# A recurrent second layer on one core: nine of ten GpSimd sums per round moved to VectorE

## The chip, the cores and the metric

The kernel runs on one core of a Trainium2 chip, in float32 throughout. The metric is the device time of one execution in microseconds (us). The core's engines are TensorE (PE in the profile), VectorE (DVE), ScalarE (ACT), GpSimd (POOL) and SyncE (SP), which issues most of the DMAs. Each engine runs its own list of instructions in order; between engines only semaphores order the work.

## What is computed

The reference has two layers, over a batch of 8 sequences of 256 tokens and 512 channels. The first is a transformer block (self attention, cross attention, feed-forward). The change doesn't touch it. The second is a recurrent block with a time mix and a channel mix. Cut to what matters:

```
xa  = layernorm(x)                        # xaT: channels on partitions
sx  = previous token of xa - xa
xxx = tanh((xa + sx * maa_x) @ maa_w1) @ maa_w2      # five mixes
x_f = xa + sx * (maa_stack_f + xxx_f)     # f = k, w, v, r, g
w = exp(-exp(..)); r, k, v = x_r @ Wr.T, x_k @ Wk.T, x_v @ Wv.T; g = silu(x_g @ Wg.T)
for each token: out = r . (u * k v + S);  S = k v + w * S
og = group_norm(out);  x1 = x + (og * g) @ Wo.T
xc = layernorm(x1);  sx2 = previous token of xc - xc
out = x1 + sigmoid((xc + sx2 * maa_r) @ Wfr.T) * (square(relu((xc + sx2 * maa_k) @ Wfk.T)) @ Wfv.T)
```

## The kernel before

The second layer (`recurrent_block`) is a pipeline over batches with five stages, "lfasd": `l` is the layer norm ahead of the first layer's feed-forward, `f` that feed-forward (64 matmuls of 256 columns and 32 of 512 per batch), `a` the time mix up to r, k, v, w and g, `s` the scan with the group norm and the output product, `d` the channel mix. `pipeline` (L1476) calls each engine's `body` once per round. In round i the stages work on batches i, i-1, i-2, i-3 and i-4, so that rounds 2 and 3 lack the late stages, rounds 4 to 7 have all five, round 8 lacks `l`, round 9 also lacks `f`, and rounds 10 and 11 are the end. In the trace round 2 begins at about 850 us, round 3 at 970, round 4 at 1113, and rounds 4 to 8 take some 141 us each, to 1819.

The order of work in a round is written out by hand, separately for each engine. A tensor of one batch lies as 128 partitions x 4 x 256, so that one sum over it is one instruction of 128x1024 elements.

**GpSimd** (L1706 to L1755) makes ten such sums per round, each behind a wait on another engine's semaphore: `xf = x2 + b2` (L1731); `sx` from `xaT` (L1736); the five mix sums `mixed += xaT` (`add_xa`, L1714), the first four in a loop; `o += bv`, the scan's output plus the bonus of the same token (L1744); then the fifth mix sum; `o *= sq`, the group norm's rstd (L1750); and `sx2` from `xcT` (L1753). Where stage `f` is absent (round 9), VectorE makes the fifth mix sum (L2354) and `o *= sq` (L2373) itself; in round 10 also `sx2` (L2285).

**VectorE** (L2110 to L2409) runs the scan in eight steps of a batch, `step(s, 0)` to `step(s, 7)` (L2124): a product (L2133) of 128x2048, two scans (L2144) of 128x1028 and a product (L2151) of 128x2048. Steps 0 to 2 of a batch come at the end of one round, steps 3 to 7 in the next. Between the steps stand the small operations: `shift` (L2154) makes `sx * (stack + xxx)` into `mixed`, from PSUM; L2313 makes the input of the first mix product from `sx`; L2357 is k * r for the bonus; L2364 the gate; L2368 the bonus times v; L2379 the gated output; `take_ff2` (L2240) adds a feed-forward product from PSUM into `xf` and so frees one of two banks; `mix_channel` (L2271) uses `sx2`.

**TensorE** (L1957) runs through the products of all stages in one list. In the tail of a round it makes the feed-forward product L1795, then the product `dev` of `o` (L1847, waits on `o_made`, L2065), the first half of the gate product (L1828, waits on the fifth mix sum, L2053), the product `var` (L1847), the second half of the gate, the bonus in two halves (L1847, L2078; the second half needs the bank that VectorE's first L2364 frees), a feed-forward product (L1805), the sums of a scan step (`add_rows`, L1897) and the output product. The k product waits on mix sum 1 (L2008), the v product on mix sum 3 (L2034).

**ScalarE** squares the deviations, makes rstd (L2644, L2647), the gate's tanh (L2527), then waits for `o*sq` (L2651) and scales it (L2653). SyncE reads `o` back from memory (L1653) once the scan's rows are stored, loads the scan's rows `ks`, `ws`, `rs`, `vs` and the weights, which are streamed anew in each round.

Of the kernel before, what the change touches and what calls it, by code (L numbers as in the profile page):

```python
# [6 lines left out]
ALU = mybir.AluOpType  # L7
# [1202 lines left out]
def recurrent_block(nc, sems, T, keep, x2_dram, x3_dram, out_dram, early_ring_in, early_x3_out):  # L1210


    with ExitStack() as ctx:
# [493 lines left out]
        def _(pool):  # L1707
# [3 lines left out]
            def add_xa(a, f):  # L1711
                pool.wait_ge(*emptied(a, f"mix{f}", 1))
                alone(pool)
                nc.gpsimd.tensor_tensor(mixed[:, f % 2, :, :], mixed[:, f % 2, :, :], xaT[:, :, 1:SEQ + 1], ALU.add)\  # L1714
                    .then_inc(mix_made.sem, 1)

            def body(t):
# [15 lines left out]
                if a is not None:  # L1733
                    pool.wait_ge(*emptied(a, "xaT", 1))
                    alone(pool)
                    nc.gpsimd.tensor_tensor(sx[:, :, :], xaT[:, :, 0:SEQ], xaT[:, :, 1:SEQ + 1], ALU.subtract)\  # L1736
                        .then_inc(sx_made.sem, 1)
                    for f_ in range(4):
                        add_xa(a, f_)
                if s is not None and f is not None:  # L1740
                    for tally in (bv_in, o_in):
                        pool.wait_ge(tally.sem, tally.at(s, 1))
                        alone(pool)
                    nc.gpsimd.tensor_tensor(o[:, :, :], o[:, :, :], bv[:, :, :], ALU.add).then_inc(o_made.sem, 1)  # L1744
                if a is not None and f is not None:
                    add_xa(a, 4)
                if s is not None and f is not None:
                    pool.wait_ge(rstd_made.sem, rstd_made.at(s, 1))
                    alone(pool)
                    nc.gpsimd.tensor_tensor(o[:, :, :], o[:, :, :], sq[:, :, :], ALU.mult).then_inc(y_made.sem, 1)  # L1750
                    pool.wait_ge(*emptied(s, "xcT", 1))
                    alone(pool)
                    nc.gpsimd.tensor_tensor(sx2[:, :, :], xcT[:, :, 0:SEQ], xcT[:, :, 1:SEQ + 1], ALU.subtract)\  # L1753
                        .then_inc(sx2_made.sem, 1)
# [356 lines left out]
        def _(dve):  # L2111
# [158 lines left out]

            def mix_channel(s):  # L2271
# [22 lines left out]
            def body(t):  # L2294
# [28 lines left out]
                if a is not None:  # L2323
                    shift_pair(a, (0, 1), 1)
                if d is not None and d != LAST:
                    add_channel(d)
# [406 lines left out]
```

## Time and profile before

| | |
|---|---|
| median of 3 runs | 2054.96 us (2052.15 to 2056.28) |
| the profiled execution | 2053.13 us, its span 2051.4 us |
| PE busy | 1899.5 us (93%) |
| DVE busy | 1445.3 us (70%) |
| ACT busy | 870.5 us (42%) |
| POOL busy | 486.0 us (24%) |
| POOL in the second layer: L1714 | 39 instructions, 114.2 us |
| L1731, L1736, L1744, L1750, L1753 | 7, 8, 6, 6, 6 instructions |

How to read it: busy time is the sum over the instructions of an engine, and a share of the span is an average over two layers with different limits. The median of all runs lies 1.8 us above the profiled execution. In a row of a timeline or a group, L1714 is a line of the kernel, `b_mixed<-b_mixed,b_xaT` the tensor written and those read, `128x1024` partitions by elements, and "[3.95 <-POOL b_mixed L1714]" the idle time ahead of the instruction and what ended it. Records of neighbouring instructions can overlap by some 0.1 us. "issue" is waiting for nothing that the profile shows. A row of the windows gives: stretch, its length, then busy us and (x instructions) of PE, PEld (weight loads), DVE, ACT and POOL, the granted TensorE clock as a share of full speed, the DMA share and GB/s.

### The profile page before, as it was taken

The numbers are of one execution on the slowest core, as the hardware profiler recorded it, in microseconds if no ns is written. First come the engines' busy times: TensorE is split into PE (matmuls) and PEld (weight loads), VectorE is DVE, ScalarE is ACT, GpSimd is POOL, SyncE is SP. The second block draws the span as 40 slices with busy tenths as digits, with TensorE's granted clock in tenths as the row PEclk, the third lists the DMA queues.
The fourth block names the chain that finished last, engine by engine and source line by source line (L and its number), as shares of the span: only waits on it lengthen the run. The fifth ranks groups of instructions, "written<-read, shape, count | busy, mean of one in ns | idle before, by whom it ended". The sixth has DMA issues, their size and how long they took to land.

```text
span 2051.4 us, 29340 instructions
## 1 busy us (share of the span) xinstructions
PE 1899.5 (93%) x11284; PEld 1293.4 (63%) x11284; DVE 1445.3 (70%) x2472; ACT 870.5 (42%) x2068; POOL 486.0 (24%) x234
## 2 busy tenths in 40 slices
PE   6789999999999999989799999999999999997577
PEld 4566666667666666566576666766767766766343
DVE  3366666767666635236968978888889889789972
ACT  2466666666666656221243243242332431321222
POOL 2233333343433322120221211212202202112000
PEclk9799999999999999999899999999999999999788
DMA  7000000101001021643554464563644644625330
GB/s 216 19 9 27 11 27 12 32 7 36 27 11 47 32 88 42 209 168 113 180 189 157 154 203 141 187 204 126 209 169 162 213 160 138 205 101 166 113 103 31
DMA packets 152788, 227.80 MB, mean 111 GB/s; under 512 B 24185, under 2 KB 72057, under 8 KB 152649
## 3 DMA queue, kind: packets, MB, share of 16 engines
q1 hardware_dynamic: 127272, 205.07, 30.4%
q10 hardware_dynamic: 25376, 20.86, 3.2%
q8 instruction: 90, 1.47, 0.3%
q14 instruction: 50, 0.40, 0.1%
HBM read 183.94 MB, written 41.96 MB: 110 GB/s over the span
## 4 chain that ended last, share of the span: by engine, by line
PE 44%; DVE 6%; DMA 3%; issue 2%; ACT 2%; POOL 1%; ACTq 1%; DVEq 0%; SPq 0%; POOLq 0%
PE b_f_bank L1805 9%; PE b_f_bank L1795 9%; PE b_a_bank L1828 7%; PE b_c_bank L1838 7%; PE b_c_bank L1828 3%; DVE b_ring L2144 2%; PE b_y_bank L1897 2%; PE b_a_bank L1861 2%; DMA b_o<-b_o_all 1%; POOL b_mixed L1714 1%; DVE b_ring L2133 1%; DMA b_o_all<-b_osum 1%; PE b_f_bank L1925 1%; ACTq L2466 1%; PE b_a_bank L1882 1%
## 5 line engine op out<-in xcount | busy, mean ns | idle before, releaser
L406 POOL TENSOR_TENSOR a_prob<-a_prob,a_rowinv 128x1024 f32<-128x1024 f32 x128 | 242.2, 1893 | 504.7 <-DVE a_rowinv L861 504.6
L1093 ACT ACTIVATE a_prob<-a_score,a_low 128x256 f32<-128x256 f32 x512 | 253.6, 497 | 228.1 <-DVE a_low L853 228.1
L2144 DVE TENSOR_TENSOR_SCAN b_ring<-b_ws,b_ring 128x1028 f32<-128x1028 f32 x128 | 312.4, 2482 | 3.6 <-ACT b_ring L2449 0.7
L1795 PE MATMUL b_f_bank<-k_hT_early,k_w_early 128*128 128x256 f32 x896 | 208.9, 388 | 3.9 <-DVE k_enc_early L2248 2.5
L1805 PE MATMUL b_f_bank<-k_w_early 128*128 128x512 f32 x448 | 204.3, 607 | 0.0
L853 DVE CUSTOM_DVE_ANT_0 a_score<-a_score,a_fill 128x256 f32<-128x256 f32 x512 | 196.6, 446 | 4.8 <-DVE a_score L840 0.2
L1795 PEld LDWEIGHTS b_f_bank<-k_hT_early,k_w_early 128*128 128x128 f32 x896 | 169.4, 192 | 40.7 <-issue 18.3
L840 DVE SCALAR_TENSOR_TENSOR a_score<-a_S,a_mask 128x1024 f32<-128x1024 f32 x128 | 150.7, 1219 | 49.5 <-PE a_S L600 49.5
L1714 POOL TENSOR_TENSOR b_mixed<-b_mixed,b_xaT 128x1024 f32<-128x1024 f32 x39 | 114.2, 2945 | 299.9 <-DVE b_mixed L2170 279.6
L2133 DVE TENSOR_TENSOR b_ring<-b_ks,b_vs 128x2048 f32<-128x2048 f32 x64 | 180.4, 2820 | 3.2 <-issue 3.2
L833 DVE TENSOR_SCALAR a_ctxT<-a_O,a_vec 128x256 f32<-128x256 f32 x64 | 31.0, 484 | 207.6 <-PE a_O L630 207.6
L2151 DVE TENSOR_TENSOR b_ring<-b_ring,b_rs 128x2048 f32<-128x2048 f32 x64 | 153.8, 2403 | 2.2
L1805 PEld LDWEIGHTS b_f_bank<-k_w_early 128*128 128x128 f32 x448 | 84.8, 193 | 102.1 <-issue 101.7
L614 PEld LDWEIGHTS a_S<-k_ident,a_prob 128*128 128x128 f32 x1024 | 120.6, 145 | 30.9 <-issue 15.3
L614 PE MATMUL a_S<-k_ident,a_prob 128*128 128x128 f32 x1024 | 127.9, 280 | 9.9 <-DVE a_score L840 9.9
L1105 ACT ACTIVATE a_probT<-a_S 128x1024 f32<-128x1024 f32 x128 | 128.5, 1007 | 7.8 <-PE a_S L614 7.8
L1828 PE MATMUL b_a_bank<-b_mixed,b_shared 128*128 128x256 f32 x512 | 117.5, 389 | 7.9 <-DMA b_shared<-in_Wk_dram 3.5
L501 PE MATMUL a_G<-k_hT_early,k_w_early 128*128 128x256 f32 x512 | 118.7, 386 | 4.9 <-ACT k_hT_early L1047 3.7
L1828 PEld LDWEIGHTS b_a_bank<-b_mixed,b_shared 128*128 128x128 f32 x512 | 99.8, 196 | 23.1 <-issue 7.7
L2508 ACT ACTIVATE k_w_early<-b_f_bank,k_b_col 128x256 f32<-128x256 f32 x112 | 46.9, 470 | 156.5 <-PE b_f_bank L1795 156.4
L501 PEld LDWEIGHTS a_G<-k_hT_early,k_w_early 128*128 128x128 f32 x512 | 96.5, 193 | 21.4 <-issue 8.8
L1093 ACT ACTIVATION_READ_ACCUMULATOR a_prob<-a_score,a_low 128x1 f32 x512 | 96.8, 189 | 0.0
(201 smaller groups left out, 3004.0 us busy)
## 6 DMA issues: line engine op xcount, KB each, us to landing
k_w_early<-in_w_dram SPq DMA_DIRECT2D x64, 1024.0 KB, 5.5
b_vs<-b_v_all SPq DMA_DIRECT2D x32, 512.0 KB, 5.0
b_shared<-in_Wv_dram SPq DMA_DIRECT2D x8, 1024.0 KB, 6.1
b_shared<-in_Wk_dram SPq DMA_DIRECT2D x8, 1024.0 KB, 5.3
b_shared<-in_Wo_dram SPq DMA_DIRECT2D x8, 1024.0 KB, 6.1
b_shared<-in_Wfk_dram SPq DMA_DIRECT2D x8, 1024.0 KB, 7.9
b_shared<-in_Wfv_dram SPq DMA_DIRECT2D x8, 1024.0 KB, 5.3
b_w_all<-b_wT ACTq DMA_DIRECT2D x8, 514.0 KB, 4.4
```

The source lines that it names most:

```text
L406: nc.gpsimd.tensor_tensor(two, two, inv.to_broadcast([P, 2 * TT, SEQ]), ALU.mult)\
L501: last = nc.tensor.matmul(bank[:, m * SEQ:(m + 1) * SEQ], w[:, c, col + m * P:col + (m + 1) * P], actT[:, c, :], start=(c == 0), stop=(c = ...
L614: last = nc.tensor.transpose(S[:, j, k * SEQ + a * P:k * SEQ + (a + 1) * P], prob[:, HPG * (g % 2) + j, a * SEQ + k * P:a * SEQ + (k + 1) ...
L840: last = nc.vector.scalar_tensor_tensor(out=score[:, 2 * pair:2 * pair + 2, :], in0=S[:, 2 * pair:2 * pair + 2, :], scalar=-SCORE_SCALE, i ...
L853: last = nc.vector.tensor_tensor_reduce(sc, sc, fill[:, at, a * SEQ:(a + 1) * SEQ], 1.0, 3.0e38, ALU.add, ALU.min, low[:, HPG * g + j, a:a ...
L1093: last = nc.scalar.activation(prob[:, slot, a * SEQ:(a + 1) * SEQ], score[:, j, a * SEQ:(a + 1) * SEQ], ACT.Exp, bias=low[:, head, a:a + 1 ...
L1795: last = nc.tensor.matmul(bank[:, m * SEQ:(m + 1) * SEQ], w1[:, cg, col_:col_ + P], hTf[:, cg, :], start=(cg == 0), stop=(cg == CG - 1))
L1805: last = nc.tensor.matmul(bank[:, :], f1T(quarter, cg)[:, at * P:(at + 1) * P], w2[:, cg, :], start=(cg == 0), stop=(cg == CG - 1))
L1828: last = nc.tensor.matmul(tile(name, k)[:, m * SEQ:(m + 1) * SEQ], w[:, c, (2 * k + m) * P:(2 * k + m + 1) * P], act[:, c, :], start=(c == ...
L2133: nc.vector.tensor_tensor(slot[:, :, :, 1:SEQ + 1], ks[:, :, :].unsqueeze(1).to_broadcast([P, JCOLS, IROWS, SEQ]), vs[:, u // 2 % 2, u % 2 ...
L2144: last = nc.vector.tensor_tensor_scan(x_, flat(ws[:, :, :]), x_, 0.0, ALU.mult, ALU.add)
L2151: nc.vector.tensor_tensor(x_, x_, rs[:, :, :].unsqueeze(1).to_broadcast([P, JCOLS, IROWS, SEQ]), ALU.mult).then_inc(weighed.sem, 1)
```

## The change

VectorE makes nine of the ten sums, each directly behind the operation whose result it needs: `sx` after step 3, mix sums 1 and 2 after the second pair of shifts of mixes 0 and 1, mix sums 3 and 4 after those of mixes 2 and 3 (ahead of step 7), the fifth mix sum after its shift, `o += bv` after L2357 and ahead of step 0, `o *= sq` after step 0 and ahead of the gate, `sx2` ahead of `mix_channel`. GpSimd keeps `xf = x2 + b2` (L1731). The semaphores stay the same ones; the waits that stood in GpSimd's queue stand in VectorE's. No other engine's list changes.

```diff
--- before.py
+++ after.py
@@ -1708,12 +1708,6 @@
             nc.gpsimd.memset(wT[:, :, 0:1], 0.0)
             xf_made.done(pool, 1)
 
-            def add_xa(a, f):
-                pool.wait_ge(*emptied(a, f"mix{f}", 1))
-                alone(pool)
-                nc.gpsimd.tensor_tensor(mixed[:, f % 2, :, :], mixed[:, f % 2, :, :], xaT[:, :, 1:SEQ + 1], ALU.add)\
-                    .then_inc(mix_made.sem, 1)
-
             def body(t):
                 l, f, a, s, d = t.stages()
 
@@ -1730,28 +1724,6 @@
                         alone(pool)
                     nc.gpsimd.tensor_tensor(xf[:, :, :], x2[:, :, :], b2_all[:, :, :].to_broadcast([P, TT, DM]), ALU.add)\
                         .then_inc(xf_made.sem, 1)
-                if a is not None:
-                    pool.wait_ge(*emptied(a, "xaT", 1))
-                    alone(pool)
-                    nc.gpsimd.tensor_tensor(sx[:, :, :], xaT[:, :, 0:SEQ], xaT[:, :, 1:SEQ + 1], ALU.subtract)\
-                        .then_inc(sx_made.sem, 1)
-                    for f_ in range(4):
-                        add_xa(a, f_)
-                if s is not None and f is not None:
-                    for tally in (bv_in, o_in):
-                        pool.wait_ge(tally.sem, tally.at(s, 1))
-                        alone(pool)
-                    nc.gpsimd.tensor_tensor(o[:, :, :], o[:, :, :], bv[:, :, :], ALU.add).then_inc(o_made.sem, 1)
-                if a is not None and f is not None:
-                    add_xa(a, 4)
-                if s is not None and f is not None:
-                    pool.wait_ge(rstd_made.sem, rstd_made.at(s, 1))
-                    alone(pool)
-                    nc.gpsimd.tensor_tensor(o[:, :, :], o[:, :, :], sq[:, :, :], ALU.mult).then_inc(y_made.sem, 1)
-                    pool.wait_ge(*emptied(s, "xcT", 1))
-                    alone(pool)
-                    nc.gpsimd.tensor_tensor(sx2[:, :, :], xcT[:, :, 0:SEQ], xcT[:, :, 1:SEQ + 1], ALU.subtract)\
-                        .then_inc(sx2_made.sem, 1)
             pipeline(pool, body)
 
         @block.tensor
@@ -2268,6 +2240,11 @@
                 nc.vector.scalar_tensor_tensor(out=x_, in0=flat(o[:, :, :]), scalar=0.5, in1=x_, op0=ALU.mult,
                                                op1=ALU.add).then_inc(out_made.sem, 1)
 
+            def add_xa(a, f):
+                dve.wait_ge(*emptied(a, f"mix{f}", 1))
+                nc.vector.tensor_tensor(mixed[:, f % 2, :, :], mixed[:, f % 2, :, :], xaT[:, :, 1:SEQ + 1], ALU.add)\
+                    .then_inc(mix_made.sem, 1)
+
             def mix_channel(s):
 
                 dve.wait_ge(sx2_made.sem, sx2_made.at(s, 1))
@@ -2307,6 +2284,9 @@
                 if s is not None:
                     step(s, 3)
                 if a is not None:
+                    dve.wait_ge(*emptied(a, "xaT", 1))
+                    nc.vector.tensor_tensor(sx[:, :, :], xaT[:, :, 0:SEQ], xaT[:, :, 1:SEQ + 1], ALU.subtract)\
+                        .then_inc(sx_made.sem, 1)
                     dve.wait_ge(sx_made.sem, sx_made.at(a, 1))
                     dve.wait_ge(g_out.sem, g_out.at(a, 0))
                     for cg in range(CG):
@@ -2322,6 +2302,8 @@
                     gate_channel(d)
                 if a is not None:
                     shift_pair(a, (0, 1), 1)
+                    add_xa(a, 0)
+                    add_xa(a, 1)
                 if d is not None and d != LAST:
                     add_channel(d)
                 if s is not None:
@@ -2334,6 +2316,8 @@
                     take_ff2(f, 0)
                 if a is not None:
                     shift_pair(a, (2, 3), 1)
+                    add_xa(a, 2)
+                    add_xa(a, 3)
                 if s is not None:
                     if f is None and a is not None:
                         step(s, 6)
@@ -2349,13 +2333,17 @@
                 if a is not None:
                     for k in range(2):
                         shift(a, 4, k)
-                    if f is None:
-                        dve.wait_ge(*emptied(a, "mix4", 1))
-                        nc.vector.tensor_tensor(mixed[:, 0, :, :], mixed[:, 0, :, :], xaT[:, :, 1:SEQ + 1], ALU.add)\
-                            .then_inc(mix_made.sem, 1)
+                    add_xa(a, 4)
                     dve.wait_ge(*emptied(a, "r", 1))
                     nc.vector.tensor_tensor(mixed[:, 1, :, :], kT[:, :, :], rT[:, :, :], ALU.mult).then_inc(rk_made.sem, 1)
+                    if s is not None and f is not None:
+                        for tally in (bv_in, o_in):
+                            dve.wait_ge(tally.sem, tally.at(s, 1))
+                        nc.vector.tensor_tensor(o[:, :, :], o[:, :, :], bv[:, :, :], ALU.add).then_inc(o_made.sem, 1)
                     step(a, 0)
+                    if s is not None and f is not None:
+                        dve.wait_ge(rstd_made.sem, rstd_made.at(s, 1))
+                        nc.vector.tensor_tensor(o[:, :, :], o[:, :, :], sq[:, :, :], ALU.mult).then_inc(y_made.sem, 1)
                     if f is None:
                         step(a, 1)
                     for k in range(2):
@@ -2399,6 +2387,9 @@
                 if f is not None:
                     take_ff2(f, 4)
                 if s is not None and f is not None:
+                    dve.wait_ge(*emptied(s, "xcT", 1))
+                    nc.vector.tensor_tensor(sx2[:, :, :], xcT[:, :, 0:SEQ], xcT[:, :, 1:SEQ + 1], ALU.subtract)\
+                        .then_inc(sx2_made.sem, 1)
                     mix_channel(s)
                 if f is not None:
                     for i in range(5, 8):
```

## Rows read from the trace of the kernel before

**Rows 1.** Windows, rounds 4 to 8 (columns as in the section on time)

```profile
1113.00:1254.30 141.30, 139.41 (x809) 96.23 (x808) 119.46 (x108) 47.10 (x89) 27.44 (x10) 1.00 0.54 175
...
sum 706.30, PE 696.85 PEld 480.92 DVE 593.81 ACT 230.82 POOL 140.32; mean PE 139.37 PEld 96.18 DVE 118.76 ACT 46.16 POOL 28.06
```

**Rows 2.** PE's waits in rounds 4 to 8: us in total, times, longest

```profile
PE b_a_bank L1828 <- POOL b_mixed L1714: 5.6, 5, 1.1
PE b_a_bank L1847 <- DVE b_z_gT L2364: 3.1, 5, 0.6
```

**Rows 3.** Chain in round 4, from 1196 to 1222: start us, us, what

```profile
1200.91 3.16 POOL b_mixed L1714
...
1204.12 3.72 PE b_a_bank L1828 x16
...
1213.75 0.70 DVE b_z_gT L2364
...
1214.50 1.13 PE b_a_bank L1847 x4
```

**Rows 4.** POOL timeline, round 4: start, us, instruction, [idle <-releaser]

```profile
1198.61 2.35 POOL L1744 TENSOR_TENSOR b_o<-b_o,b_bv 128x1024 f32<-128x1024 f32 x1 [19.44 <-DMA b_o<-b_o_all]
...
1213.38 2.35 POOL L1750 TENSOR_TENSOR b_o<-b_o,b_sq 128x1024 f32<-128x1024 f32 x1 [9.31 <-ACT b_sq L2647]
```

**Rows 5.** DVE's timeline in round 4

```profile
1194.17 0.17 DVE L2191 RECIPROCAL b_rstd<-b_std 128x2 f32<-128x2 f32 x1 [6.19 <-ACT b_std L2420]
...
1197.30 2.16 DVE L2162 SCALAR_TENSOR_TENSOR b_mixed<-b_a_bank,k_vec_b,b_sx 128x128 f32<-128x128 f32 x8 [1.92 <-PE b_a_bank L1873]
1199.37 2.67 DVE L2357 TENSOR_TENSOR b_mixed<-b_kT,b_rT 128x1024 f32<-128x1024 f32 x1
1201.96 4.25 DVE L2133 TENSOR_TENSOR b_ring<-b_ks,b_vs 128x2048 f32<-128x2048 f32 x1
```

**Rows 6.** DVE timeline, round 9, where it makes such a sum already

```profile
1893.77 1.22 DVE L2354 TENSOR_TENSOR b_mixed<-b_mixed,b_xaT 128x1024 f32<-128x1024 f32 x1
1894.91 1.22 DVE L2357 TENSOR_TENSOR b_mixed<-b_kT,b_rT 128x1024 f32<-128x1024 f32 x1
```

**Rows 7.** DVE L2133 over the whole run: ns min/median/max

```profile
L2133 DVE TENSOR_TENSOR b_ring<-b_ks,b_vs x64: 2274/2284/4254, 919.7 to 1980.2; 128x2048 f32<-128x2048 f32 x64
```

**Rows 8.** PE's timeline in round 2: waits, and what ran after them

```profile
924.03 9.81 PE L1828 MATMUL b_a_bank<-b_mixed,b_Wg 128*128 128x256 f32 x32 [3.95 <-POOL b_mixed L1714]
...
935.40 3.60 PE L1805 MATMUL b_f_bank<-k_w_early 128*128 128x512 f32 x8
...
949.60 5.38 PE L1795 MATMUL b_f_bank<-k_hT_early,k_w_early 128*128 128x256 f32 x16 [2.50 <-DVE k_enc_early L2248]
```

**Rows 9.** DVE's timeline in rounds 2 and 3

```profile
928.36 2.29 DVE L2151 TENSOR_TENSOR b_ring<-b_ring,b_rs 128x2048 f32<-128x2048 f32 x1
...
984.48 3.80 DVE L2151 TENSOR_TENSOR b_ring<-b_ring,b_rs 128x2048 f32<-128x2048 f32 x1
```

**Rows 10.** PE's timeline in round 3

```profile
1025.01 2.07 PE L1861 MATMUL b_a_bank<-b_t,b_maa_w 32*128 32x256 f32 x8 [7.48 <-DVE b_mixed L2170]
...
1060.52 1.99 PE L1847 MATMUL b_c_bank<-b_o,k_dev_head 128*128 128x256 f32 x8 [1.93 <-POOL b_o L1744]
```

**Rows 11.** DVE's timeline in round 9, steps 6 and 7

```profile
1868.06 3.75 DVE L2133 TENSOR_TENSOR b_ring<-b_ks,b_vs 128x2048 f32<-128x2048 f32 x1
1871.85 6.35 DVE L2144 TENSOR_TENSOR_SCAN b_ring<-b_ws,b_ring 128x1028 f32<-128x1028 f32 x2
...
1882.76 4.49 DVE L2144 TENSOR_TENSOR_SCAN b_ring<-b_ws,b_ring 128x1028 f32<-128x1028 f32 x2
```

**Rows 12.** PE's timeline in round 9, wait for step 6

```profile
1880.58 1.08 PE L1897 MATMUL b_y_bank<-b_ring,k_same_quad 128*32 128x128 f32 x32 [3.69 <-DVE b_ring L2151]
```

**Rows 13.** PE's timeline in round 9, third idle time

```profile
1914.98 1.27 PE L1847 MATMUL b_a_bank<-b_mixed,k_u_head 128*128 128x256 f32 x4 [1.94 <-DVE b_z_gT L2364]
1916.19 1.93 PE L1897 MATMUL b_y_bank<-b_ring,k_same_quad 128*32 128x128 f32 x32
```

## The prediction

> **What bounds the kernel now.** I cut the second layer into rounds with the windows first. Rounds 4 to 8 are alike: 706.3 us in all, TensorE busy for 696.9 of it at full granted clock, VectorE for 593.8 [rows 1]. TensorE is the bound there, VectorE has 141.3 - 119.5 = 21.8 us idle per round. Whatever VectorE gains in these rounds is therefore worth nothing by itself; only what TensorE waits for counts. Its list of waits for the same stretch is short [rows 2]: 1.1 us per round for GpSimd's fifth mix sum (L1714), 0.6 us per round for VectorE's gate (L2364), and one of 0.2 us. All five waits on L1714 are this one, so mix sums 1 to 4, `sx`, `sx2` and `o*sq` are waited for by nobody on TensorE. The chain of waits shows where the two sit: the tail of the round, between the fifth mix sum and the bonus product [rows 3]. Rounds 2, 3 and 9 are different: there VectorE's scan steps are waited for, for 7.48 us in round 3 and 3.69 us in round 9 [rows 10, 12], and GpSimd's fifth sum alone for 3.95 us in round 2 [rows 8].
>
> **The price of one sum.** GpSimd takes 2.35 us where nothing is in its way [rows 4]. VectorE makes the same shape in 1.22 us, and the next starts 1.14 us after it [rows 6]. Nine of these put 9 x 1.14 = 10.3 us per round on VectorE.
>
> **What VectorE gets back.** Its product L2133 takes 2.28 us, but 4.25 us when a GpSimd sum is under way [rows 5, 7]; a pair of scans takes 4.49 us, but 6.35 us beside two sums [rows 11]; L2357 takes 2.67 us instead of 1.22 [rows 5, 6]. One engine waits for the other's instruction to end. The Trainium skill says the same of the shared port ("SBUF — State Buffer", Who interferes with whom). In a round like 4, three L2133, one scan pair, L2357 and one more operation of its shape meet the nine sums: I estimate 2.0 + 1.5 + 2.0 + 1.9 + 1.4 + 1.4 = 10.2 us. So VectorE's load stays nearly as it is and fits in its time; even if nothing came back, 10.3 us would fit in 21.8. The tenth sum stays on GpSimd and still holds VectorE up once a round.
>
> A rule speaks against the change: the Trainium skill ("Perfetto Trace Analysis", Optimizing Scalar/DVE Operations) has saturated VectorE hand work over to other engines. VectorE idles for 21.8 us a round here, so the rule does not bite; were VectorE the bound and nothing given back, five rounds would grow by 5 x 10.3 = 52 us, against the 7.5 of the sum below.
>
> **The tail of rounds 4 to 8, on round 4's times.**
> - Before: TensorE starts the deviation product at about 1201.0, when GpSimd's `o+bv` (1198.61 + 2.35) is done, which is also when it is free; GpSimd then makes the fifth mix sum until 1204.07, and the gate product starts at 1204.12 [rows 3, 4].
> - After: VectorE's L2162 ends at 1199.46; then the fifth mix sum (1199.5), L2357 (1200.6) and only then `o+bv` (1201.8 to 1203.0) [rows 5, 6]. The deviation product starts at 1203.05, 2.05 us later: a new wait. It takes 1.8 us, so the gate product, whose input is long ready, starts at 1204.9: 0.8 us later than before.
> - ScalarE's variance and rstd follow TensorE and come 0.8 us later too. GpSimd started `o*sq` at 1213.38 [rows 4], so VectorE starts it at 1214.1 and ends at 1215.3. Step 0 isn't late: it starts at 1202.9 without the 1.97 us of holding and ends at 1212.1. `y` is ready at 1215.3 against 1215.7 before, so ScalarE isn't late.
> - But `o*sq` now stands ahead of the gate L2364, which started at 1213.75 and now starts at 1215.2. The second bonus product waits for it: 1214.50 becomes 1215.95. So the delay is 1.45 us, and it stays to the end of the round, because TensorE never catches up. VectorE does not carry its own delay over: it waits for ScalarE for 6.19 us before the next tail [rows 5].
>
> Five rounds by 1.5 us: **+7.5 us**.
>
> **Other placements.** `sx` (L1736) runs after step 3 for 1.14 us on VectorE instead of overlapping it; step 3's L2151 was held for 1.5 us in return (3.80 against 2.29) [rows 9]. Mix sums 1 to 4 follow their shifts, ahead of steps 5 and 7: +2.3 us for each pair, against the holding of 1.5 + 1.9 that went. `sx2` puts 1.14 us ahead of two second-layer sums that free PSUM banks; TensorE has about 1 us in hand there, so I cost it at zero, and at most 0.2 us per round if that cover is gone. VectorE's own waits now stand in its queue: the one on the load of `o` is met at 1198.6 in round 4, 3 us before it is asked for [rows 4]. No DMA is added or moved; queues of SP and POOL lose nothing but the nine sums.
>
> **Round 2** loses the 3.95 us wait, and the half-clock stretch after it. But the scan step that follows (L2151 ends at 930.65) then decides the gate and the second bonus product [rows 9]: VectorE's L2364 ends near 930.7, TensorE's second-layer product of 935.40 starts near 931.9 [rows 8]. That is 3.5 us earlier, or 1.8 if the clock falls in the new 2.9 us wait: after a wait of 2.50 us sixteen matmuls took 5.38 us [rows 8] against 3.7 at full clock. With 0.4 us at the first mix sum I take **-3.0 us** (bounds -2.2 and -4.0).
>
> **Round 3**: VectorE sets the pace until the 7.48 us wait [rows 10]. `sx` and step 3 give -0.4, the first pair of mix sums 2.3 - 3.4 = -1.1: -1.4 in all. The tail costs less than later (the input `o` came late, TensorE waited 1.93 us already [rows 10]): +0.6. Sum **-0.8 us**.
>
> **Round 9**: the same two terms, -0.4 and 2.3 - 1.5 - 1.9 = -1.1, ahead of a chain of steps that VectorE carries to the end [rows 11, 12]: **-1.6 us**. Rounds 10 and 11 have no such sums.
>
> **The clock.** The trace shows no cost of the new 2.05 us wait, so it is bounded. Nothing: after 1.93 us the matmuls ran at full clock [rows 10]. Up to 1.7 us each: after 2.50 us they ran at half clock (1.2 instead of 2.4 GHz) [rows 8]. Between them, after 1.94 us, the y products took 1.93 us instead of 1.1 [rows 13], about 1.0 us in all. I take one loss of 1.0 us in five rounds, since 1.93 and 1.94 are the nearest rows and differ; range 0 to 8.5.
>
> **Sum:** 7.5 - 3.0 - 0.8 - 1.6 + 1.0 = +3.1 us. It is made against the profiled execution (2053.1 us, span 2051.4); the median of three runs is 2055.0, so I forecast 2058.
>
> **Rivals.**
> - *Clock lost in most tails* (slower). The place is the deviation product's wait; the price 1.0 to 1.7 us each, decided once the wait is over about 2 us. Four or five losses give 7.5 - 5.4 + 4 to 8.5 = +6 to +11, 2061 to 2066. For it: rows 8 and 13; against: rows 10. Chance 0.24.
> - *The holding was the true price* (faster). If round 2 gives its full 4.0 with the clock kept and more, round 3 and 9 give the 3.4 us of each pair in full, and the tail costs 0.7 us per round because the gate isn't pushed back: 3.5 - 4 - 2.5 - 2.5 = -5.5, 2049.5. Against it: L2364 stands behind `o*sq` in VectorE's queue, whatever happens before. Chance 0.10.
> - *VectorE becomes the bound* or the load of `o` comes later than 1201.8: its queue, step 0 behind it, would stop. +5 us or more, 2060 to 2065. Against it: 21.8 us idle, 3 us in hand. Chance 0.09.
> - *Nothing moves* (the two sides cancel, GpSimd's waits were the whole cost): within 2 us of 2055. Chance 0.12.
> - The forecast: 0.45.
>
> A measurement of this kernel can tell about 0.2% (4.1 us) from no change. My forecast is inside it, with its upper third outside, so it gives 0.15 to slower; with the rivals: faster 0.12, same 0.46, slower 0.42. The range leaves out the far ends: 2050 to 2066.
>
> **What would show it.** In rounds 4 to 8, TensorE's waits: about 2.0 us at L1847 for `o+bv` and 1.3 us for L2364, none for a mix sum; round length 143.0. L2133 at 2.28 us at all but one place, no scan pair at 6.35 us except beside the tenth sum. GpSimd has seven sums left. PEclk in rounds 4 to 8 near 1.0; a tenth below 1.0 there is the first rival. Round 2 shorter by 3 us. I am wrong if TensorE's new waits sum to under 2.5 us per round, or if VectorE is never idle in one.

## The result, and the profile after

| | before | after |
|---|---|---|
| median of 19 runs each | 2053.71 us (2052.02 to 2058.07) | 2058.93 us (2055.31 to 2066.32) |
| the profiled execution | 2053.13 us | 2064.26 us, its span 2062.5 us |

The ratio is 1.0027, 95% interval 1.0018 to 1.0037: slower by 5 us. That is little, but the interval leaves out 1. The profiled execution lies 5.3 us above its own kernel's median, and after's runs spread over 11 us where before's spread over 6. So a term read in this one profile has to be held against the other runs before it is believed.

The page of after, busy time by engine:

```profile
## 1 busy us (share of the span) xinstructions
PE 1903.0 (92%) x11284; PEld 1298.6 (63%) x11284; DVE 1450.2 (70%) x2537; ACT 870.7 (42%) x2068; POOL 307.7 (15%) x169
```

GpSimd lost 65 instructions and 178 us. VectorE gained 65 instructions and 4.9 us. That is all its load grew. In lines of after, L2245 is a mix sum, L2342 `o+bv`, L2346 `o*sq`, L2338 the old L2357, L2352 the gate (old L2364), L2105 the old L2133, L2123 the old L2151, L1819 the deviation and bonus products (old L1847), L1800 the old L1828, L1877 the old L1905.

Windows of after on rounds 4 to 8, the same columns as [rows 1]:

```profile
1096.70:1239.50 142.80, 139.34 (x813) 96.50 (x809) 119.60 (x118) 47.14 (x91) 3.15 (x1) 1.00 0.55 174
...
1382.20:1526.70 144.50, 141.04 (x814) 97.62 (x809) 119.62 (x118) 47.15 (x90) 3.33 (x1) 0.99 0.52 172
...
1669.50:1813.00 143.50, 140.04 (x804) 96.76 (x801) 116.06 (x111) 43.92 (x88) 3.44 (x1) 0.99 0.51 168
sum 716.30, PE 699.00 PEld 483.83 DVE 594.28 ACT 232.38 POOL 17.57; mean PE 139.80 PEld 96.77 DVE 118.86 ACT 46.48 POOL 3.51
```

Five rounds take 716.3 us instead of 706.3. VectorE is busy for 594.28 us of them against 593.81 [rows 1]: nine more sums a round, and no more load. TensorE's busy time grew only in the two rounds with a granted clock of 0.99.

What TensorE waits for in rounds 4 to 8 of after, in the form of [rows 2]:

```profile
PE b_c_bank L1819 <- DVE b_o L2342: 10.6, 5, 2.1
PE b_a_bank L1819 <- DVE b_z_gT L2352: 6.3, 5, 1.3
```

No mix sum is waited for any more. `o+bv` is, for 2.1 us in every round, and the wait for the gate doubled from 0.62 to 1.27 us. VectorE's timeline of round 4 shows why:

```profile
1195.00 2.16 DVE L2134 SCALAR_TENSOR_TENSOR b_mixed<-b_a_bank,k_vec_b,b_sx 128x128 f32<-128x128 f32 x8 [1.93 <-PE b_a_bank L1845]
1197.19 1.23 DVE L2245 TENSOR_TENSOR b_mixed<-b_mixed,b_xaT 128x1024 f32<-128x1024 f32 x1
1198.34 1.22 DVE L2338 TENSOR_TENSOR b_mixed<-b_kT,b_rT 128x1024 f32<-128x1024 f32 x1
1199.47 1.22 DVE L2342 TENSOR_TENSOR b_o<-b_o,b_bv 128x1024 f32<-128x1024 f32 x1
1200.61 2.29 DVE L2105 TENSOR_TENSOR b_ring<-b_ks,b_vs 128x2048 f32<-128x2048 f32 x1
...
1211.62 1.23 DVE L2346 TENSOR_TENSOR b_o<-b_o,b_sq 128x1024 f32<-128x1024 f32 x1 [1.62 <-ACT b_sq L2638]
1212.76 1.28 DVE L2352 SCALAR_TENSOR_TENSOR b_z_gT<-b_z_gT,b_a_bank 128x512 f32<-128x512 f32 x2
```

`o+bv` stands third behind the shifts, and the gate stands behind `o*sq`, which waits for ScalarE. Nothing is held: the fifth sum, L2338 and `o+bv` take 1.22 us each, where L2357 took 2.67 beside GpSimd [rows 5]. TensorE, rounds 4, 6 and 8, at the deviation product:

```profile
1200.74 1.99 PE L1819 MATMUL b_c_bank<-b_o,k_dev_head 128*128 128x256 f32 x8 [2.13 <-DVE b_o L2342]
...
1486.28 3.38 PE L1819 MATMUL b_c_bank<-b_o,k_dev_head 128*128 128x256 f32 x8 [2.12 <-DVE b_o L2342]
...
1773.51 3.63 PE L1819 MATMUL b_c_bank<-b_o,k_dev_head 128*128 128x256 f32 x8 [2.13 <-DVE b_o L2342]
```

The same wait, three times. After it the eight matmuls take 1.99 us, or 3.4 to 3.6 us at a lower clock: in rounds 6 and 8 full clock was lost. The window on the slow matmuls of round 6 has the granted clock, 0.50 of full speed:

```profile
1486.70:1490.10 3.40, 3.40 (x10) 2.66 (x9) 3.27 (x2) 1.00 (x2) 0.00 (x0) 0.50 0.42 154
```

**Where the 11.1 us of span went.** I cut both traces at the first matmul of the longest run (x32) of the feed-forward product L1805 (L1777 in after) in each round, so that round 4 goes from 1099.0 to 1240.5 before. The first layer and its end gave +1.3, round 2 -4.0, round 3 +0.4, rounds 4 to 8 +9.8, and rounds 9 to 11 +3.6 us. A clean round took 142.77 us against 141.49, which is 5 x 1.28 = 6.4; the two rounds without full clock took 1.7 more each, 3.4 together. The medians differ by 5.2 us only: 11.1 less the 3.6 of the last rounds (which other profiles of the same list do not show, see below) and the 1.3 of a layer that the change does not touch would be 6.2.

### The profile page after: what moved, and what is told of

It reads as the page before. It is cut to its first block, busy times and chain, and to the rows that moved or that the text cites. A ratio compares the mean times of both kernels' runs of the same rounds, so it can differ in the third digit from the quotient of the medians.

```text
span 2062.5 us, 29275 instructions
## 1 busy us (share of the span) xinstructions
PE 1903.0 (92%) x11284; PEld 1298.6 (63%) x11284; DVE 1450.2 (70%) x2537; ACT 870.7 (42%) x2068; POOL 307.7 (15%) x169
## 4 chain that ended last, share of the span: by engine, by line
PE 44%; DVE 7%; DMA 3%; issue 2%; ACT 2%; ACTq 1%; SPq 0%; DVEq 0%
PE b_f_bank L1777 9%; PE b_f_bank L1767 8%; PE b_c_bank L1810 8%; PE b_a_bank L1800 7%; PE b_c_bank L1800 3%; DVE b_ring L2116 2%; PE b_y_bank L1869 2%; DMA b_vs<-b_v_all 2%; PE b_a_bank L1833 2%; PE b_c_bank L1819 1%; DVE b_ring L2105 1%; DMA b_o_all<-b_osum 1%; PE b_f_bank L1897 1%; ACTq L2457 1%; PE b_a_bank L1854 1%
## 5 line engine op out<-in xcount | busy, mean ns | idle before, releaser
L2116 DVE TENSOR_TENSOR_SCAN b_ring<-b_ws,b_ring 128x1028 f32<-128x1028 f32 x128 | 298.0, 2370 | 3.6 <-ACT b_ring L2440 0.7
L1777 PE MATMUL b_f_bank<-k_w_early 128*128 128x512 f32 x448 | 204.4, 607 | 0.0
L2123 DVE TENSOR_TENSOR b_ring<-b_ring,b_rs 128x2048 f32<-128x2048 f32 x64 | 148.7, 2323 | 2.6 <-DMA b_rs<-b_r_all 0.5
L1777 PEld LDWEIGHTS b_f_bank<-k_w_early 128*128 128x128 f32 x448 | 84.9, 194 | 102.4 <-issue 102.0
L2105 DVE TENSOR_TENSOR b_ring<-b_ks,b_vs 128x2048 f32<-128x2048 f32 x64 | 146.3, 2286 | 0.4 <-issue 0.4
L1725 POOL TENSOR_TENSOR k_enc_early<-k_x_early,k_b_all 128x1024 f32<-128x1024 f32 x7 | 22.9, 3271 | 821.8 <-DMA x_all<-k_enc_early 821.8
L1800 PE MATMUL b_a_bank<-b_mixed,b_shared 128*128 128x256 f32 x512 | 118.3, 391 | 7.1 <-DMA b_shared<-in_Wk_dram 3.4
L1800 PEld LDWEIGHTS b_a_bank<-b_mixed,b_shared 128*128 128x128 f32 x512 | 100.4, 197 | 22.5 <-issue 7.2
```

Of the source, the lines that this page charges most:

```text
L1777: last = nc.tensor.matmul(bank[:, :], f1T(quarter, cg)[:, at * P:(at + 1) * P], w2[:, cg, :], start=(cg == 0), stop=(cg == CG - 1))
L1800: last = nc.tensor.matmul(tile(name, k)[:, m * SEQ:(m + 1) * SEQ], w[:, c, (2 * k + m) * P:(2 * k + m + 1) * P], act[:, c, :], start=(c == ...
L2105: nc.vector.tensor_tensor(slot[:, :, :, 1:SEQ + 1], ks[:, :, :].unsqueeze(1).to_broadcast([P, JCOLS, IROWS, SEQ]), vs[:, u // 2 % 2, u % 2 ...
L2116: last = nc.vector.tensor_tensor_scan(x_, flat(ws[:, :, :]), x_, 0.0, ALU.mult, ALU.add)
```

## The experiments

All edits are to the changed kernel. Ratios are against the kernel before, run beside each on the same chip. "Round" is a round of rounds 4 to 8, cut as above. "OBV" stands for the wait on `bv` and `o` with `o += bv`, "OSQ" for the wait on rstd with `o *= sq`.

**1. `o+bv` first (e1_o_first).**

```diff
                     for k in range(2):
                         shift(a, 4, k)
+                    OBV
                     add_xa(a, 4)
                     ...
-                    OBV
                     step(a, 0)
```

> The change with one line moved: VectorE makes o += bv ahead of the fifth mix sum instead of behind that sum and L2357. Theory (order in the tail): o is loaded before the shift of the fifth mix ends, so the sum is done when TensorE is free and its wait of 2.1 us at the deviation product goes; the wait for the gate stays near 1.3 us. Rounds 4 to 8: 142.8 - 1.9 = about 140.9 us each and full clock there; time 2047 to 2051, ratio to the kernel before 0.997 to 0.999. Rival (load): VectorE has too much to do, the place of one sum changes nothing but moves the wait to the gate product; rounds stay at 142.8, ratio 1.002 to 1.003.

Measured: 2048.54 us, ratio 0.9971 (0.9954 to 0.9989). The wait at the deviation product is gone in all rounds, and rounds take 140.3 to 141.2 us but for one of 142.88. The other wait grew:

```profile
PE b_a_bank L1819 <- DVE b_z_gT L2352: 9.6, 5, 2.1
```

TensorE arrives earlier, and the gate still stands behind `o*sq`, so this wait, expected to stay near 1.3 us, grew by 0.4 to 0.8 us. Full clock, expected throughout, was lost after it twice: in round 3 (a wait of 2.26 us) and in round 5 (2.09 us, the round of 142.88), but not after the 2.10 and 2.08 us of rounds 4 and 8. Moving one operation by two places in one queue is worth 0.6% (1.0027 to 0.9971).

**2. `o+bv` and `o*sq` back to GpSimd (e4_two_back).** The two blocks go back into GpSimd's list, in their old order; the other seven sums stay on VectorE.

> The change with o += bv and o *= sq given back to GpSimd; the other seven sums stay on VectorE. Theory (order in the tail): both new waits go, and the old wait of 1.1 us for the fifth mix sum stays away, since GpSimd no longer makes it: rounds 4 to 8 at 140.2 to 140.5 us each, waits of TensorE there 0.6 us for the gate alone; ratio 0.994 to 0.997 (2041 to 2048 us). Rival (load): seven more sums on VectorE still cost something in each round, and GpSimd's sums hold VectorE up again: rounds at 141.5 or more, ratio 1.000 to 1.002.

Measured: 2040.30 us, ratio 0.9935 (0.9922 to 0.9948), rounds of 139.2 to 140.6. Its waits in rounds 4 to 8 (L1828 is its L1819, L2354 its gate):

```profile
PE b_a_bank L1828 <- DVE b_z_gT L2354: 3.1, 5, 0.6
PE b_c_bank L1828 <- POOL b_o L1731: 0.6, 1, 0.6
```

Without the mix sums in front of it GpSimd has `o+bv` ready nearly in time, and the wait for the gate is the 0.6 of before. The ratio is a little better than expected (0.994 to 0.997). A clean round, 140.03 us, is still 0.3 us longer than the best version's below: the deviation product takes 1.99 us there as after a wait, not the 1.89 us of a product that follows without a break.

**3. The tail alone (e5_tail_only).** Only the fifth mix sum, `o+bv` and `o*sq` on VectorE; the other six go back to GpSimd.

> Only the tail's three sums move to VectorE (fifth mix sum, o += bv, o *= sq); sx, mix sums 1 to 4 and sx2 stay on GpSimd. Theory (order in the tail): rounds 4 to 8 as slow as with the whole change, +1.3 us each and some with a clock loss of 1.7 us on top; round 2 still 3.6 us shorter; ratio 1.002 to 1.004. Rival (load): most of the loss comes from the six other sums; rounds near 141.5, ratio below 1.000.

Measured: 2061.68 us, ratio 1.0034 (1.0021 to 1.0047): as slow as the whole change. Rounds of 142.77 us (141.90 in round 8), waits of 2.13 and 1.26 us, and one round of 144.46 in which full clock was lost. Round 2 was 5.6 us shorter than before, not the 3.6 expected; 1.7 of it is the clock in its first product, which ran in 7.14 us instead of before's 8.83.

**4. The head alone (e6_head_only).** The reverse: `sx`, mix sums 1 to 4 and `sx2` on VectorE, the tail's three on GpSimd.

> Only sx, mix sums 1 to 4 and sx2 move to VectorE; the tail's three stay on GpSimd. Theory (order in the tail): rounds 4 to 8 unchanged at 141.5 us with the old waits of 1.1 and 0.6 us, round 2 shorter by 0.4 us only; ratio 0.999 to 1.001. Rival (load): these six sums carry most of the loss, rounds at 142 or more; ratio 1.002 or more.

Measured: 2053.71 us, ratio 0.9993 (0.9984 to 1.0001): no change beyond its interval. Rounds of 140.5 to 141.9 us but for one of 146.06, with the waits of before:

```profile
PE b_a_bank L1814 <- POOL b_mixed L1735: 6.6, 5, 2.2
PE b_a_bank L1833 <- DVE b_z_gT L2360: 3.1, 5, 0.6
PE b_c_bank L1833 <- POOL b_o L1731: 2.4, 2, 1.9
```

Four of the five waits for the fifth sum (its L1735) are the 1.1 us of [rows 2]. In the long round TensorE waited 1.9 us for GpSimd's `o+bv` and then 2.2 us for the fifth sum behind it; after the first wait the matmuls kept full clock (1.99 us), after the second they ran at half clock (5.41 us for sixteen, against 3.72). Round 2 was 2.2 us shorter, of which 1.7 is again the clock in its first product. Experiments 3 and 4 together put the whole price on the tail, and there on order, since the tail's work is the same in 3 and in the best version below.

**5. All nine on VectorE, in a better order (e3_both).** `o+bv` ahead of the fifth sum, and `o*sq` between the two halves of the gate.

```diff
                     step(a, 0)
-                    OSQ
                     ...
                     for k in range(2):
                         ...
                         nc.vector.scalar_tensor_tensor(out=x_, in0=x_, scalar=1.0, in1=tile("g", k)[:, :],
                                                        op0=ALU.add, op1=ALU.mult).then_inc(empty_sem("g"), 1)
+                        if k == 0:
+                            OSQ
```

> All nine sums on VectorE as in the change, but two of them placed otherwise: o += bv ahead of the fifth mix sum, o *= sq behind the first of the two gates L2364. Theory (order in the tail): VectorE's speed at these sums was never the trouble, so with nine sums on VectorE the rounds 4 to 8 fall to 139.8 to 140.3 us, as with the two sums given back to GpSimd; TensorE waits 0.6 us for the gate only; ratio 0.993 to 0.996 (2040 to 2046 us). Rival: the two sums belong on GpSimd, VectorE can't hold both without one of them being late; rounds at 140.8 or more and ratio 0.997 or more.

Measured: 2038.99 us (2038.63 to 2043.58), ratio 0.9924 (0.991 to 0.9937), a little better than expected (0.993 to 0.996) and the fastest version, with e12; e4's interval overlaps theirs. A clean round takes 139.73 us. VectorE's timeline of its round 4 (L2339 is `o+bv`, L2349 the gate, L2353 `o*sq`):

```profile
1193.89 1.22 DVE L2339 TENSOR_TENSOR b_o<-b_o,b_bv 128x1024 f32<-128x1024 f32 x1
1195.02 1.22 DVE L2245 TENSOR_TENSOR b_mixed<-b_mixed,b_xaT 128x1024 f32<-128x1024 f32 x1
1196.16 1.22 DVE L2342 TENSOR_TENSOR b_mixed<-b_kT,b_rT 128x1024 f32<-128x1024 f32 x1
...
1206.54 0.69 DVE L2349 SCALAR_TENSOR_TENSOR b_z_gT<-b_z_gT,b_a_bank 128x512 f32<-128x512 f32 x1
1207.14 1.22 DVE L2353 TENSOR_TENSOR b_o<-b_o,b_sq 128x1024 f32<-128x1024 f32 x1
1208.28 0.68 DVE L2349 SCALAR_TENSOR_TENSOR b_z_gT<-b_z_gT,b_a_bank 128x512 f32<-128x512 f32 x1
```

TensorE, same stretch, and the sum of the windows on its five rounds:

```profile
1195.27 1.89 PE L1819 MATMUL b_c_bank<-b_o,k_dev_head 128*128 128x256 f32 x8
...
1207.28 1.13 PE L1819 MATMUL b_a_bank<-b_mixed,k_u_head 128*128 128x256 f32 x4 [0.62 <-DVE b_z_gT L2349]
```

```profile
sum 698.30, PE 694.32 PEld 481.51 DVE 593.67 ACT 232.54 POOL 15.78; mean PE 138.86 PEld 96.30 DVE 118.73 ACT 46.51 POOL 3.16
```

VectorE's busy time is that of before and of after to within 0.1%, in five rounds that are 8 us shorter than before and 18 shorter than after. Its load decided nothing; the place of two operations did. TensorE idles for 4.0 us in five rounds instead of the 9.5 of before; the gate is waited for, 0.6 us in three rounds and 0.94 and 0.84 in two.

**6 and 7. One of the two alone on GpSimd (e9_sq_back, e10_obv_back).** OSQ, or OBV, moved to GpSimd's list, all else as after.

> The change with o *= sq alone given back to GpSimd. It separates the two new waits. Theory: the wait of 2.1 us at the deviation product stays, the wait for the gate goes back from 1.3 to 0.6 us; rounds 4 to 8 at 142.1 us where the clock holds, and the clock is still lost in some; ratio 1.000 to 1.003. Rival (the second wait follows from the first): the gate wait stays near 1.3 us and the rounds at 142.8.

> The change with o += bv alone given back to GpSimd. Theory: the wait at the deviation product goes; the wait for the gate grows to about 1.7 us, because o *= sq still stands ahead of it; rounds 4 to 8 at 140.8 us; ratio 0.996 to 0.999. Rival: the deviation product still waits, since GpSimd's sum and VectorE's hold each other up; rounds at 142 or more.

Measured: with OSQ back 2057.41 us, 1.0009 (1.0 to 1.0018); clean rounds 142.12, that is 0.65 less than after, and waits of 2.13 and 0.62 us. Three rounds lost full clock (143.8 us). With OBV back 2047.93 us, 0.9968 (0.9956 to 0.998); rounds of 140.5 to 141.4, the gate is waited for, 1.6 to 1.9 us, and in one round GpSimd's `o+bv`, 0.36 us. No round lost full clock. So `o*sq` ahead of the gate costs 0.65 us a round, or 1.0 to 1.5 where TensorE comes early (e10, e1).

**8. The same change with the wait shorter or longer (e13, e11, e14).** e13 puts `o+bv` between the fifth sum and L2338, a place earlier than after. e11 puts one dummy product ahead of it, which writes `sx2` (free there), e14 two:

```diff
+                        for dummy in (sx, sx2):
+                            nc.vector.tensor_tensor(dummy[:, :, :], kT[:, :, :], rT[:, :, :], ALU.mult)
                         OBV
```

> The change with o += bv between the fifth mix sum and L2357, so that the deviation product's wait is about 1.0 us instead of 2.1. Theory (the clock is lost the more often the longer the wait): no loss in rounds 3 to 8; these rounds take 141.6 us all alike; ratio 0.997 to 1.000. Rival (the losses don't depend on this wait): one to three rounds of the profile with the deviation product at 2.7 to 3.8 us instead of 2.0.

> The change with one more product of 128x1024 on VectorE ahead of o += bv (it writes sx2, which is made anew before it is read; nothing else changes). The wait at the deviation product becomes 2.1 + 1.15 = 3.3 us in rounds 3 to 8. Theory of the clock (a wait of 2.1 us loses it in some rounds, one of 2.5 us or more always does): every one of these rounds runs its next matmuls at half clock, so rounds 4 to 8 take 142.8 + 1.15 + 1.7 = 145.6 us, all alike; ratio 1.008 to 1.011. Rival (the losses in two rounds of the profile have another cause, as the weights or the DMAs of those rounds): most rounds take 143.9, a few 145.7; ratio 1.004 to 1.007.

> The change with two more products of 128x1024 on VectorE ahead of o += bv (they write sx and sx2, which are made anew before they are read). The deviation product's wait becomes 4.4 us. Theory: with a wait this long the clock is lost in all six rounds; rounds 4 to 8 take 142.8 + 2.3 + 1.7 to 1.9 = about 147 us; ratio 1.012 to 1.016. Rival: as with 3.3 us, two rounds or more of six keep the full clock, at 145 us.

Each of these has six such waits, rounds 3 to 8. "Lost" counts those after which the eight matmuls took 2.7 us or more instead of 1.99. The medians are of 10, 19, 4 and 2 runs, the rest is from one profile per kernel:

| kernel | wait, us | lost | round, clean / lost | median us | ratio |
|---|---|---|---|---|---|
| e13 | 0.99 | 0 of 6 | 141.64 / none | 2050.27 | 0.9979 (0.9969 to 0.9988) |
| after, e5, e9 | 2.13 | 2, 1 and 3 of 6 | 142.77 / 144.46 (after) | 2058.93 (after) | 1.0027 (1.0018 to 1.0037) |
| e11 | 3.26 | 4 of 6 | 143.91 / 145.6 to 146.6 | 2074.85 | 1.0092 (1.0075 to 1.0108) |
| e14 | 4.40 | 6 of 6 | none / 146.73 | 2085.15 | 1.0145 (1.0121 to 1.0169) |

TensorE in round 4 of e14:

```profile
1208.73 3.66 PE L1819 MATMUL b_c_bank<-b_o,k_dev_head 128*128 128x256 f32 x8 [4.40 <-DVE b_o L2345]
1212.22 3.62 PE L1800 MATMUL b_a_bank<-b_mixed,b_Wg 128*128 128x256 f32 x16
```

The first dummy adds its own 1.14 us to a clean round. A loss adds 1.7 us, and in rounds 7 and 8 of e11 2.7 to 2.8 us: in round 7 the eight matmuls took 3.78 us and the gate product's sixteen behind them 4.62 instead of 3.62. My expectation for e11 that a wait longer than about 2.5 us always loses the clock fell, though its ratio lay in the range: at 3.26 us two of six kept full clock. At 2.13 us 6 of 18 lost it. e5 and e9 are other kernels with the same wait, and one profile of each is few; the order of the four lines is what is shown, not the odds themselves, and what decides between two equal waits stays open.

**9. The second broadcast load of round 9 later (e12_second_part_later).** In the profile of after, two transfers of round 9 took longer from issue to landing than before:

```profile
b_r_all<-b_rT ACTq DMA_DIRECT2D x1, 512.0 KB, 7.8
b_o_all<-b_osum ACTq DMA_DIRECT2D x4, 128.0 KB, 4.9
```

Before, the same rows of the DMA issues:

```profile
b_r_all<-b_rT ACTq DMA_DIRECT2D x1, 512.0 KB, 5.3
b_o_all<-b_osum ACTq DMA_DIRECT2D x4, 128.0 KB, 2.9
```

The load of `o` can only start behind these stores. In after the store of `r` was issued 1.2 us behind the two loads of `vs`, before 2.9 us behind them, so that more of it ran beside them. So e12 takes e3 and moves the second of them behind the load of `o`:

```diff
-                def load_begin():
+                def load_begin(parts=(0, 1)):
                 ...
-                    load_part(a, 0)
-                    load_part(a, 1)
+                    for part in parts:
+                        load_part(a, part)
                 ...
                 if a is not None and f is None:
-                    load_begin()
+                    load_begin((0,))
                 ...
                     sp.dma_start(o[:, :, :], o_dram[s, :, :].rearrange("(c p) t -> p c t", p=P)).then_inc(o_in.sem, 16)
+                if a is not None and f is None:
+                    load_part(a, 1)
```

> The kernel with all nine sums on VectorE in the better order, and in round 9 the second of two loads of vs issued behind the load of o. It asks where round 9's gain went. Theory (transfers collide): in the changed kernel r's store and the four stores of the scan's rows land 2.5 and 2.0 us later than before, because they now overlap the two loads of vs; with one of these moved, the stores land in 2.7 to 3.5 us, o comes some 2 us earlier against the round's start, TensorE's wait for it falls from 4.8 to about 3 us, and what follows the last full round takes 246 to 248 us instead of 250; ratio 0.990 to 0.992. Rival: the stores are slow for another reason; the wait for o stays at 4 us or more and the end at 249 us or more.

Measured: 2039.39 us, 0.9922 (0.9906 to 0.9938), e3's time again. In its profile the stores landed in 3.8 and 2.8 us, the wait for `o` was 1.09 us (e3 4.80), and rounds 9 to 11 took 244.8 us against e3's 250.0. That looks like the theory, but the edit is not shown to have done it: e4, whose list for round 9 has both loads in the old place, had stores of 5.2 and 3.0 us, a wait of 0.94 us and 244.5 us. What goes with the late stores in all 13 profiles is the clock of the `r` product ahead of them. In the five where its 32 matmuls ran in 7.17 us at full clock (after, e1, e3, e13, e14) the stores took 7.4 to 7.8 and 4.7 to 4.9 us; in the eight where part of them ran at half clock (8.8 to 8.9 us, before and e12 among them) 3.8 to 6.4 and 2.7 to 3.1 us. Whether the earlier `r` meets the loads of `vs` or something else is not separated, and the median shows no gain.

## Why the prediction held, and where it did not

The median, 2058.93, is 0.9 us from the forecast of 2058, and the mechanism in the tail is the one forecast. Part of the closeness is luck. The forecast was a growth of 3.1 us on a median of 2055.0; the growth was 5.2 us on one of 2053.7. Its terms erred in both directions, and the one profile overstates the last of them.

- **Rounds 4 to 8, the tail: right.** The deviation product waits 2.13 us for `o+bv` (forecast 2.05), the gate is waited for 1.27 us (1.3), and no mix sum is. A clean round grew by 1.28 us instead of 1.5. The waits alone grew by 1.67 (3.40 less 1.73); the difference is that before has one more break in TensorE's stream per round, of 0.27 us beyond the listed wait (last section), and 0.1 us more of gaps too short for the list.
- **What VectorE gets back: right.** L2105 took 2281 to 2293 ns over all 64, never the 4.25 us of [rows 5]:

```profile
L2105 DVE TENSOR_TENSOR b_ring<-b_ks,b_vs x64: 2281/2286/2293, 921.9 to 1991.0; 128x2048 f32<-128x2048 f32 x64
```

  The load stayed. The Trainium skill ("SBUF — State Buffer", Who interferes with whom) has a VectorE instruction with two inputs in SBUF contend with a GpSimd instruction that reads SBUF. The trace agrees: with the nine sums off GpSimd the longest of the 64 is 2.29 us. But e6 shows that relief of that kind is worth nothing while TensorE is the bound.
- **The clock: mechanism right, size wrong.** I took one loss of 1.0 us. The profile had two in rounds 4 to 8, of 1.7 and 1.6 us. The rival "clock lost in most tails" did not happen at this wait; it did in e11 and e14.
- **Round 2: right in kind, undersized.** -4.0 us against -3.0, the end of the range that was given for full clock kept. The gate product starts without a wait (7.17 us for 32 matmuls instead of 9.81 [rows 8]), and the new wait, for VectorE's gate behind the scan step, is there, but did not cost the clock:

```profile
920.88 7.17 PE L1800 MATMUL b_a_bank<-b_mixed,b_Wg 128*128 128x256 f32 x32
...
931.76 1.13 PE L1819 MATMUL b_a_bank<-b_mixed,k_u_head 128*128 128x256 f32 x4 [2.85 <-DVE b_z_gT L2352]
932.73 3.60 PE L1777 MATMUL b_f_bank<-k_w_early 128*128 128x512 f32 x8
```

- **Round 3: wrong, -0.8 became +0.4.** The tail cost 0.4 us, less than the 0.6 forecast. What failed is the gain of 1.4 us ahead of it, of which 0.1 us was left when the tail began. After an earlier wait of 3.38 us, as long as before, TensorE was at half clock in both kernels, but in after already in the eight matmuls that follow at once (2.08 us instead of 1.13), before only in the product behind them. VectorE's next shift waits for the eight, now 1.44 us instead of 0.50. The later wait shrank from 7.48 to 6.61 us, but it ended only 0.4 us earlier in the round, and the feed-forward product at half clock behind it took 6.34 us instead of 6.06. This is no accident of one profile: the eight matmuls took 2.07 or 2.08 us in all eleven kernels with `sx` and mix sums 1 to 4 on VectorE, and 1.13 us in before and e5, which have them on GpSimd. So moving the head has a price here that the prediction did not have.
- **Round 9: wrong, -1.6 became +3.6 in this profile and about nothing over many.** VectorE's chain came earlier as forecast, and the gate product with it, by 2.4 us. The next thing that TensorE needed was `o` from memory, and it arrived when it had before. The step that failed is that I counted the gain to the end of the chain without asking which load came last there:

```profile
1905.21 1.88 PE L1877 MATMUL b_c_bank<-b_bv,k_dev_head 128*128 128x512 f32 x4
1911.46 3.78 PE L1877 MATMUL b_c_bank<-b_o,k_dev_head 128*128 128x512 f32 x4 [4.37 <-DMA b_o<-b_o_all]
1915.03 4.50 PE L1800 MATMUL b_a_bank<-b_mixed,b_Wg 128*128 128x256 f32 x16
```

  The wait for `o` before was 1.63 us, and after this one of 4.37 us the clock was at half: the product of `o` took 3.78 us instead of 1.98, and the sixteen gate matmuls behind it 4.50 instead of 3.62. So the variance product started 2.7 us later in the round than before, and VectorE's `o*sq`, which waits for its result, 2.7 us later too. That is most of the +3.6. The list of rounds 9 to 11 is the same in after, e1, e3, e4, e9, e10, e11, e13 and e14, and there they took 244.5 to 250.0 us, 246.1 in the median, against the 245.9 of before's one profile. So neither -1.6 nor +3.6 is what this term is worth; it is near nothing.
- **What is left for the clock (an estimate).** With 6.4 for the clean rounds 4 to 8, -4.0, +0.4 and 0.2 for the end, the sum is 3.0 us without a loss of clock. The medians differ by 5.2, which leaves 2.2 us, one loss or two in a typical run.
- **The rival "the holding was the true price"** fell for this order (slower, not faster), by the argument put against it, the gate behind `o*sq`, and by `o+bv` in third place, which costs more (e1). With both operations in other places its sign came true: e3 is 0.76% faster than before. "VectorE becomes the bound" did not happen either: it idles for 23 us of round 4 (142.80 less 119.60), and its `o+bv` did not wait for the load of `o`.

**What is shown and what is argued.** Shown: the tail alone makes the slowdown (e5 against e6), both displaced operations have their part in it (e1, e9, e10), and all of it goes with their order at the same VectorE load (e3). Open: why stores land later in round 9 of after, and what decides whether a wait of 2.1 us costs the clock. That after's wide spread of runs comes from the clock is borne out by the granted clock of its 19 runs: the two at 0.968 took 2055.3 and 2055.5 us, the one at 0.963 took 2066.3. That the losses lie at this wait in each of them is argued only; the range of 11 us would be six or seven losses of 1.7.

## What to carry to other kernels

When work moves from a side engine to another in-order engine, place each piece by who waits for its result next, not directly behind the operation that it needs: here "directly behind" put the one operation that TensorE waits for third in the queue, and one that waits for ScalarE ahead of one that TensorE waits for. The same nine operations in another order turned 0.27% slower into 0.76% faster. Read the list of the bound engine's waits first: in rounds 4 to 8 only two of the ten sums had a place on it, one of them for 0.2 us in one round, and no busy time that VectorE had to spare or lacked decided the result.

## What the runs showed that I had not expected

- **A wait on TensorE can cost more than itself.** At one and the same place, 0.99 us cost the clock in none of 6 rounds, 2.13 us in 6 of 18, 3.26 us in 4 of 6, 4.40 us in all 6, mostly at 1.7 us each. At the gate, four waits of 2.08 to 2.26 us in e1 cost it twice, and six of 1.6 to 1.9 us in e10 never. Length alone does not decide: in round 2 of after, TensorE kept full clock behind a wait of 2.85 us. e14's rounds are 5.2 us longer than before's, and 1.7 us of each is the clock. That such a wait always widens the spread of a kernel's runs is not shown: after's 19 runs spread over 11 us, but the ten of e9, with the same wait, over 4, and before's over 6 to 9.
- **A break in TensorE's stream costs 0.27 us beyond the wait that the list shows.** In e3 TensorE was busy for 2.5 us less in five rounds than before (694.32 against 696.85). The same two products, without a break between them (e3) and with one (after):

```profile
1191.71 3.72 PE L1767 MATMUL b_f_bank<-k_hT_early,k_w_early 128*128 128x256 f32 x16
1195.27 1.89 PE L1819 MATMUL b_c_bank<-b_o,k_dev_head 128*128 128x256 f32 x8
```

```profile
1194.90 3.72 PE L1767 MATMUL b_f_bank<-k_hT_early,k_w_early 128*128 128x256 f32 x16
1200.74 1.99 PE L1819 MATMUL b_c_bank<-b_o,k_dev_head 128*128 128x256 f32 x8 [2.13 <-DVE b_o L2342]
```

  Without a break the second starts 3.56 us behind the first, 0.16 before the first's 3.72 us are over; with one, these 3.72 us pass in full before the wait begins. And the eight matmuls take 0.10 us more. The sixteen of the gate product show the same, 3.72 us behind a wait and 3.62 without. Before has three such breaks in a clean round (deviation product, after a gap of 0.1 us, gate product, bonus), after two, e3 one: two fewer make 0.54 us a round, 2.7 in five, where 2.5 were measured. The ends of matmuls are modelled in the profile, so how the 0.27 us fall on wait and work is the model's; that the rounds are shorter by them is measured: a clean round of e3 is 1.76 us shorter than one of before, and the listed waits make only 1.11 of it.
